# A fused embed, attention, state-space and expert kernel: maxima ahead of chain steps, the state projection behind its slot, the mask product first, a scatter awaited later

## What is computed

```python
h = concat(edges(x), (U * s @ Vt)[x_txt])
h = h + local_attention(norm(h))      # 16 heads of 16, window 128
h = h + routed_block(norm(h))         # gelu(x @ w_block) for the 288 tokens with the highest score
h = h + state_space(norm(h))          # h_t = A h_(t-1) + B u_t; A is a rotation in Fourier space
h = h + experts(norm(h))              # a shared feed-forward net, and the 2 best of 8 experts
```

## Time and profile before

| | |
|---|---|
| median of 3 runs | 2193.5 us |
| the profiled execution | 2192.07 us, of which the span is 2190.3 us |
| busy, share of the span | PE 90%, weight loads 71%, DVE 62%, ACT 49%, POOL 37% |
| granted TensorE clock, mean | 0.969 of full speed |
| passes 0 to 15 | about 69 to 1457 us; a loop pass takes 87.8 us |
| pass 16 and the hand-over to the experts | about 1457 to 1559 us |
| expert phase | about 1559 us to the end |

### The profile page before, as it was taken

The page is one execution under the profiler, slowest core; times in us unless marked ns, Lnnn a source line. Parts: engine busy times, 40 slices in busy tenths (PEclk is TensorE's granted clock), DMA queues, the critical chain, the costliest instruction groups (busy, mean ns, idle before and its releaser), DMA issues.

```text
span 2190.3 us, 44925 instructions
## 1 busy us (share of the span) xinstructions
PE 1965.9 (90%) x13651; PEld 1559.6 (71%) x13652; DVE 1350.6 (62%) x3572; ACT 1079.5 (49%) x2513; POOL 819.2 (37%) x1535
## 2 busy tenths in 40 slices
PE   2879999999999999999999999985789999999997
PEld 1546666666666666666666666653689999999997
DVE  5647668577576685775766757643455565555654
ACT  0336455455554554555545555541355455555553
POOL 3113324334243233342432333322344545454454
PEclk8789999999999999999999999996899999999998
DMA  4220211211202112112021121110333232323322
GB/s 138 65 58 9 66 45 29 65 35 45 65 15 65 44 28 65 33 47 65 15 65 43 30 65 31 35 59 8 111 84 84 44 83 47 81 48 81 48 47 40
DMA packets 81090, 116.53 MB, mean 53 GB/s; under 512 B 20965, under 2 KB 61509, under 8 KB 78725
## 3 DMA queue, kind: packets, MB, share of 16 engines
q1 hardware_dynamic: 54948, 85.34, 14.1%
q0 software_dynamic: 23360, 27.91, 7.8%
q10 hardware_dynamic: 2736, 2.76, 0.4%
HBM read 51.58 MB, written 26.71 MB: 36 GB/s over the span
## 4 chain that ended last, share of the span: by engine, by line
PE 51%; DVE 16%; issue 14%; POOL 8%; DMA 5%; ACT 4%; POOLq 0%; DVEq 0%; SPq 0%; ACTq 0%
PE ps L1780 10%; PE ps L1616 8%; POOL slot_rows L658 4%; PE ps L1493 4%; PE ps L1792 3%; PE ps L1791 3%; PE ps L1793 3%; DVE mx L1119 2%; PE ps L1582 2%; PE ps L1465 2%; DMA result<-yb,idx_o 2%; PE ps L1607 2%; PE ps L1561 2%; PE ps L1548 2%; DMA slot_rows<-pay,row_i 2%
## 5 line engine op out<-in xcount | busy, mean ns | idle before, releaser
L793 ACT ACTIVATE prob<-ps,mx 128x256 f32<-128x256 f32 (+1 forms) x768 | 295.0, 443 | 254.9 <-DVE mx L1119 240.1
L897 ACT ACTIVATE hid_hi<-ps,b 128x256 fp32r<-128x256 f32 x408 | 205.8, 504 | 286.1 <-PE ps L1780 286.1
L1119 DVE TENSOR_REDUCE mx<-ps 128x2 f32<-128x512 f32 (+1 forms) x384 | 224.5, 594 | 116.0 <-PE ps L1540 107.3
L785 ACT ACTIVATE pT<-ps 128x512 f32<-128x512 f32 (+1 forms) x384 | 205.2, 534 | 123.9 <-PE ps L1548 120.5
L1395 DVE TENSOR_TENSOR hid_lo<-hid_full,hid_hi 128x256 fp32r<-128x256 f32 x408 | 172.3, 426 | 150.7 <-ACT hid_full L900 150.1
L1539 PE MATMUL ps<-ks,qs 96*128 96x512 f32 (+1 forms) x384 | 186.7, 487 | 63.9 <-ACT prob L793 51.0
L1791 PE MATMUL ps<-w_hi,hid_hi 128*128 128x256 f32 x816 | 232.3, 285 | 0.0
L1792 PE MATMUL ps<-w_lo,hid_hi 128*128 128x256 f32 x816 | 227.9, 279 | 0.0
L1793 PE MATMUL ps<-w_hi,hid_lo 128*128 128x256 f32 x816 | 227.9, 279 | 0.0
L900 ACT ACTIVATE hid_full<-ps,b 128x256 f32<-128x256 f32 x408 | 206.2, 505 | 0.0
L1548 PE MATMUL ps<-ident,prob 128*128 128x128 f32 x1280 | 204.8, 277 | 0.0
(11 more groups left out here) (269 smaller groups left out, 4175.6 us busy)
## 6 DMA issues: line engine op xcount, KB each, us to landing
w_raw<-in_w SPq DMA_DIRECT2D x16, 1024.0 KB, 6.0
xin<-in_x SPq DMA_DIRECT2D x32, 384.0 KB, 3.6
qs<-q_hi SPq DMA_DIRECT2D x128, 96.0 KB, 2.1
ks<-k_hi SPq DMA_DIRECT2D x256, 48.0 KB, 2.1
qs<-q_lo SPq DMA_DIRECT2D x64, 96.0 KB, 2.1
ks<-k_lo SPq DMA_DIRECT2D x128, 48.0 KB, 2.1
xn_rows<-xc SPq DMA_DIRECT2D x16, 384.0 KB, 2.5
result<-h SPq DMA_DIRECT2D x16, 384.0 KB, 2.5
```

Of the source, the lines that this page charges most:

```text
L785: act.activation(pT[:, u % TB, :, k0:2, :], ps[:, 2 + u % 2, :].rearrange("p (h k q) -> p h k q", h=2, k=2)[:, :, k0:2, :], ACT.Copy).then ...
L793: ins = act.activation(prob[:, s % PB, hh, w], ps[:, s % 2, hh * 2 * P + w.start:(hh + 1) * 2 * P], ACT.Exp, bias=mx[:, s % 2, hh:hh + 1])
L897: act.activation(hid_hi[:, f], ps[:, f % 4, 0:CHUNK], ACT.Gelu_apprx_tanh, bias=b1[half][:, f:f + 1])
L1119: dve.tensor_reduce(mx[:, s % 2], sc, AX_X, ALU.max, negate=True).then_inc(max_done.sem, 1)
```

## The change

- DVE: in slots 14, 20 and 21 (`LATER`) the maxima of the unit come ahead of the chain's work; the statistics of the state-space sum move from slot 20 to 21.
- PE: the drive moves behind unit 14; the queries move ahead of the last PV product; the output product moves ahead of the PV product in slots 16 and 24; the mask product comes ahead of the score product in each bank; the first of the three products of `values_sum` moves to slot 1; `turn_chain(.., 0)` waits for bank 7 only ahead of its second half.
- Pass 16: POOL's `dispatch` moves behind the state-space work; `gate_ratio` and `slot_ranks` of the last item move to slot 30, ahead of seven of the eight upper products of the shared net; DVE's last `shared_sum` moves behind the fourth of the eight list copies, and PE waits for it ahead of the first chunk.
- Expert phase, POOL: the scatter of chunk `j - 1` is awaited behind the issue of the gather for chunk `j + 2`, in place of right behind its own issue.

```diff
+LATER = (STATE, OUT + 1, OUT + 2)
@@ POOL
-                if late:
+                if late and att:
                     dispatch(b - 2)
                 if chain:
                     chain_deviations(b - 1, 1)
                     direct_term(b - 1)
                     states(b - 1)
+                if late and not att:
+                    dispatch(b - 2)
...
-                pool.wait_ge(y_stored.sem, y_stored.at(j, 32))
-                pool.sem_inc(y_sent.sem, 1)
...
+            def rows_added(j):
+                pool.wait_ge(y_stored.sem, y_stored.at(j, 0))
+                pool.sem_inc(y_sent.sem, 1)
+
+            def rows_ahead(lo, hi):
                 with pool.Fori(lo, hi) as j:
                     gather_rows(j, 2)
+                    rows_added(j)
                     add_rows(j)
@@ ACT
+                    if first_weights and s == min(UPS):
+                        gate_ratio(b - 1)
                     for f in UPS.get(s, ()) if chain else ():
                         hidden_layer(b - 1, f)
...
-            gate_ratio(NB - 1)
@@ DVE
                     dve.wait_ge(h3_ready.sem, h3_ready.at(b, 1))
+                if s == OUT + 2:
                     chain_rows(b, 2)
...
-                    if chained:
+                    if chained and s not in LATER:
                         chain(b - 1, s)
...
                     if att:
                         unit(b, s)
+                    if chained and s in LATER:
+                        chain(b - 1, s)
...
-            shared_sum(NB - 1)
...
+                if e == 3:
+                    shared_sum(NB - 1)
@@ PE
-                    pe.matmul(dst, qs[:, r, m, i * P:(i + 1) * P], ks[:, r, :, m, keys], start=True, stop=False)
-                    pe.matmul(dst, ident_bf[:], mask_bf[:, :, c0:2 * P], start=False, stop=True
+                    pe.matmul(dst, ident_bf[:], mask_bf[:, :, c0:2 * P], start=True, stop=False)
+                    pe.matmul(dst, qs[:, r, m, i * P:(i + 1) * P], ks[:, r, :, m, keys], start=False, stop=True
                               ).then_inc(scores_done.sem, 1)
...
-                if n == 0:
-                    pe.wait_ge(hid_ready.sem, hid_ready.at(b, 0))
...
+                    if n == 0 and k == 1:
+                        pe.wait_ge(hid_ready.sem, hid_ready.at(b, 0))
...
-                if s == TURN1 + 2:
+            def drive(b):
...
+                    if head and s == TURN2 - 1:
+                        queries(b + 1)
                     if att and s == BLOCK:
-                        values_sum(b)
+                        values_sum(b, 1, NT)
...
                     if att:
                         unit(b, s)
+                    if att and s == TURN0:
+                        values_sum(b, 0, 1)
...
+                    if chained and s == TURN1 + 2:
+                        drive(b - 1)
...
+                    if last and s == min(UPS):
+                        slot_ranks(b - 1, False)
...
+            pe.wait_ge(h4_ready.sem, h4_ready.at(NB, 0))
             turn_chunk(0)
```

More of the change, by code:

```diff
@@ L1517, in values, with values_sum @@
                 ins.then_inc(proj_done.sem, 1)
-            def values_sum(b):
+            def values_sum(b, first, last):
                 pe.wait_ge(v_ready.sem, v_ready.at(b, 1))
                 pe.wait_ge(h1_ready.sem, h1_ready.at(b, 0))
-                for i in range(NT):
+                for i in range(first, last):
                     ins = pe.matmul(ps[:, 5, D:2 * D].rearrange("p (h d) -> p h d", h=NH), ones9[:], vaug[:, i, :, 0:DK],
                                     start=(i == 0), stop=(i == NT - 1))
-                ins.then_inc(sumv_done.sem, 1)
+                if last == NT:
+                    ins.then_inc(sumv_done.sem, 1)
             def unit(b, s):
@@ L1550, in unit @@
                     ins.then_inc(turned.sem, 1)
+                if s in WO:
+                    i = WO.index(s)
+                    pe.wait_ge(cxT_ready.sem, cxT_ready.at(b, i + 1))
+                    for k in range(KB):
+                        ins = pe.matmul(ps[:, 5, D:2 * D], cxT[:, k], wo[:, k], start=(k == 0), stop=(k == KB - 1))
+                    ins.then_inc(wo_done.sem, 1)
                 if PV <= s < NU + PV and (s - PV) % 2 == 1:
@@ L1577, in unit, with turn_chain @@
                     ins.then_inc(cx_turned.sem, 1)
-                if s in WO:
-                    i = WO.index(s)
-                    pe.wait_ge(cxT_ready.sem, cxT_ready.at(b, i + 1))
-                    for k in range(KB):
-                        ins = pe.matmul(ps[:, 5, D:2 * D], cxT[:, k], wo[:, k], start=(k == 0), stop=(k == KB - 1))
-                    ins.then_inc(wo_done.sem, 1)
             def tile_out(i):
                 return ps[:, 6 + i // 2, (i % 2) * D:(i % 2 + 1) * D]
-            def turn_chain(b, n, head):
+            def turn_chain(b, n, head, first=False):
+                if n == 0 and not first:
+                    pe.wait_ge(hid_ready.sem, hid_ready.at(b - 1, FB - 1))
                 pe.wait_ge(xc_ready.sem, xc_ready.at(b, n + 1))
                 pe.wait_ge(xcT_ready.sem, xcT_ready.at(b, n))
-                if n == 0:
-                    pe.wait_ge(hid_ready.sem, hid_ready.at(b, 0))
                 if n == 1:
@@ L1687, in logits, with sequence @@
                     ins.then_inc(logit_done.sem, 1)
-            def sequence(b, att, late, chained, head, first=False):
+            def sequence(b, att, late, chained, head, first=False, last=False):
                 for s in range(SLOTS):
-                    if first and s == 1:
+                    if first and not chained and s == 1:
                         pe.wait_ge(mats_read.sem, mats_read.at(0, 1))
@@ L1703, in sequence @@
                     if chained and s == TURN0:
-                        turn_chain(b - 1, 0, head)
+                        turn_chain(b - 1, 0, head, first)
                     if att:
                         unit(b, s)
+                    if att and s == TURN0:
+                        values_sum(b, 0, 1)
                     if late and s == RANKS:
@@ L1720, in sequence @@
                         turn_rows(b + 1)
-                    if head and s == TURN2 - 1:
-                        queries(b + 1)
                     if head and s == TURN2:
@@ L1746, in _ @@
             pe.wait_ge(late_loaded.sem, late_loaded.at(0, NLATE))
-            sequence(1, True, False, True, True)
+            sequence(1, True, False, True, True, first=True)
             with pe.Fori(2, NB - 1) as b:
@@ L1750, in _ @@
             sequence(NB - 1, True, True, True, False)
[L1751 to L1752 removed]
+            sequence(NB, False, True, True, False, last=True)
             for n in range(2 * NT):
```

12 lines of the change are left out of this document (6 added, 6 removed).

## The result

The changed kernel is slower: 2222.7 us (median of 4 runs, 2219.2 to 2226.4) against 2192.5 us for the kernel before (median of 4 runs, 2188.2 to 2195.5), ratio 1.014, 95% interval 1.0113 to 1.0166. The profiled execution took 2225.24 us with a span of 2223.5. The forecast was 2220.

A forecast was written before the change was run, and what follows sets the result against it. PE was taken as the bound, busy 82.12 of a pass's 87.80 us. Fourteen passes +52, passes 0 and 15 −2.5, first expert product −12.7, experts −9 gave +28 on 2192.07: 2220 us, range 2165 to 2262.

The forecast's parts named there:

- Start: Loop pass up to slot 14: shorter waits for turned rows and last hidden piece, score 14 about 0.75 us earlier.
- Drive: Loop pass, slots 14 to 16: about 4 us idle before unit 14, first edge product 3.1 us later, score 16 2.7 late.
- Mask first: Each unit's bank in a pass: 0.09 us less per wide unit, 1.7 us a pass, about 0.4 us of it counting.
- Slots 19 to 22: Loop pass: the 1.06 us wait before score 22 goes, `turn_rows` waits about 2 us, 0.7 us more to score 23.
- Slots 24 to 26: Loop pass end: output product and queries fill 1.4 us of waits, and 0.3 us of alignment goes.
- Clock: Loop pass: half-clock dip at the 4 us wait costs 1.55 us; one at `turn_rows` in six of ten passes, 0.7 us.
- Passes 0 and 15: Outside the regular loop passes: they keep the small gains, −2.5 us together (0 to −5).
- Pass 16: Moved dispatch gains 3.5 − 0.9 = 2.6 us; with moved ranks, first expert product starts 12.7 us sooner (8 to 14).
- Experts: Expert phase: PE's 10.0 us of waits for gathered rows and a 1 us clock dip go, −9 us (−4 to −11).
- No dip: Rival: the clock stays full in the loop, +20 us there and −24 outside, 2188 us; chance 0.15.
- The drive absorbed: Rival: DVE and edge products catch up before slot 20, a pass gains 2.9 us, total 2128 us; chance 0.18.
- Longer dips: Rival: PE at 1.2 GHz through slots 14 to 18 and from 22 on, +6 us a pass, 2252 us; chance 0.17.

The follow-up runs named there:

- e12: Changed kernel with the drive back ahead of unit 14 and DVE's loop order wholly as in the kernel before (LATER empty): 2129.0 us, ratio 0.971.
- e4: Kernel before with only the changes outside passes 0 to 15 (dispatch, gate ratio, ranks, shared sum, scatter): 2165.3 us, ratio 0.988.
- e8: Kernel before with only the mask product put ahead of the score product in each bank: 2183.1 us, ratio 0.996.
- e6: Changed kernel with the drive back ahead of unit 14 and DVE's slots 20 and 21 ordered as in the kernel before: 2131.4 us, ratio 0.972.
- e1: Changed kernel with the drive back ahead of unit 14 on PE, all else as changed: 2162.3 us, ratio 0.986.
- e3: Kernel before with only the drive moved behind unit 14 and DVE's products with u behind the maxima of slot 14: 2267.7 us, ratio 1.034.
- e5: Changed kernel with the drive back ahead of unit 14 and DVE's statistics of slot 21 moved behind the normalised rows (xn): 2148.2 us, ratio 0.979.
- e11: Changed kernel with only DVE's slots 20 and 21 back in the order of the kernel before, drive still behind unit 14: 2214.1 us, ratio 1.010.
- e2: Changed kernel with an extra, unawaited run of the drive ahead of unit 14, besides the one behind it: 2208.9 us, ratio 1.008.
- e9: e6 with the statistics put behind the maxima of slot 22, the sum still ahead of the maxima of slot 20: 2144.0 us, ratio 0.977.
- e7: Kernel before with only the expert phase changed, a chunk's scatter awaited behind the next gather: 2176.0 us, ratio 0.992.
- e10: e6 with the statistics put between the maxima of slots 20 and 21, the sum still ahead of both: 2130.3 us, ratio 0.971.

## Why the prediction came out

The sign, the size (2222.7 against 2220) and the mechanism at slot 14 were right. That the size came out so close is luck: the fourteen loop passes cost 57 us where 52 were forecast, passes 0 and 15 cost 7.6 us where a gain of 2.5 was, and the experts gained 19.7 where 9 were. So I go through the sum.

*The balance, in medians.* e12 has all of the change but the drive's place and DVE's order: −63.5 us. Of that, e4's ends are −27 and e8's mask order −9; the moves of projections, turned rows and value sums hold what is left, about −27, that is (87.82 − 0.36 − 85.61) × 14 = 26 by the passes, if the three add up. Putting the maxima of slots 20 and 21 first adds 31 (e6 to e1), the drive behind the unit 60 (e1 to the changed kernel), the maxima of slot 14 first nothing (e12 to e6, +2). −63.5 + 2.4 + 30.9 + 60.4 = +30.2 us. (These steps run from kernel to kernel, so they add up by construction; each by itself is a difference of two medians.)

*Start: −0.75.* From the start of the pass to score 14 it is 35.64 us, before 36.29: −0.65. Right.

*Drive: 4 us idle, the edge products 3.1 us later, score 16 2.7 late.* The wait is 3.71 us. At score 20 the changed pass is 5.7 − 0.65 = 5.1 us late; less the 2.3 us of half clock 2.8. The wait of the edge product is 1.16 us, in the 1 to 1.5 of the prediction. e3 shows it on the kernel before, e1 takes it away. Right.

*Mask first: 0.09 us a wide unit, 0.4 a pass on the path.* From the first product of a bank to the transposes it is 0.45 us now (mask at 731.04, transposes 731.49), where 0.55 was needed, and e8 has the 0.36 a pass. The Trainium skill ("TensorE: Matmul & The Clock Gate", Part 2) says that PE pulls weight loads ahead of matmuls in flight, and I had taken from it that the edit might be worth nothing. The measurement decides against that reading of it. That the saving is the bare load is read from the rows; e8 shows the size, not the cause.

*Slots 19 to 22: +0.7.* The exchange of a wait of 1.06 for one of about 2 us was right (1.85), and its price at full clock too (0.5 in the changed kernel, slot 20 to `turn_rows` 6.80 against 6.32; 0.9 in e6 against e1).

*Slots 24 to 26: −1.7.* −1.18, from `turn_rows` to the end of the pass (26.78 against 27.96). The waits for `pT` went as forecast; 0.3 us of what I had put to alignment, and 0.2 more, did not come. At full clock that makes 2.0 us a pass instead of 1.4.

*Clock: 1.55 for the dip at score 14 and 0.7 for one at `turn_rows` in six passes of ten.* The sum was right by luck, 2.25 against 2.3 us, and both terms were wrong. I took the dip's length from pass 15 (3.4 us); it was 6.8 us, of which 5.1 held work, in eleven passes (3.4 us in the first three). And the second never came. It is no invention: in e1 it comes in eight passes of twelve and costs 1.54 us, in e5 and e6, where the wait for `xn` is 0.53 us or none, never. What failed is the step that priced the two waits one by one. In the changed kernel the clock has fallen at score 14 and is whole again 23 us before the wait for `xn` begins, and this same wait leaves it alone. Whether the earlier fall is the reason, no run shows: in e1 the same wait lets the clock fall in some passes and not in others that are alike up to it. The Trainium skill ("TensorE: Matmul & The Clock Gate", "HAM oscillation") tells of a loop with waits of about 3 to 5 us whose clock falls at every one of them. The wait of 3.7 us at score 14 agrees with that, in all fourteen passes; the wait of 1.85 us is shorter than those of the page, and brought a fall in e1 in nine passes of fourteen and here in none.

Sum of a pass: 3.7 forecast, 4.35 measured in the last eleven and 2.4 to 3.6 in the first three, taken from router product to router product: 52 and 57.4 us in fourteen.

*Passes 0 and 15: −2.5.* This term failed outright, by 10 us. Of the 64.9 us lost by pass 16, 57.4 are those of the fourteen passes, 1.4 lie ahead of pass 1's router product and 6.2 in pass 15, from its router product on. In pass 15 the clock fell in a second place, for 10 us:

```profile
1500.60:1513.60 13.00, 11.76 (x53) 8.96 (x46) 5.91 (x29) 3.66 (x6) 1.39 (x2) 0.61 0.09 32
```

Before, that pass had one fall. I had carried over the loop's gains without asking what its new waits (2.5, 2.3, 1.5 and 1.2 us) would do. What brought the second fall can be read from the experiments. From router product to router product, the changed kernel and then e11, which differs from it in DVE's slots 20 and 21 alone:

```profile
1439.77:1523.42 83.65, 72.24 (x464) 52.98 (x469) 47.10 (x137) 41.70 (x94) 24.35 (x58) 0.92 0.13 44
1423.74:1501.36 77.62, 67.47 (x464) 49.11 (x469) 46.23 (x137) 41.92 (x94) 24.42 (x58) 0.98 0.15 48
```

e11 has the waits of 2.5 and 2.3 us too, and one fall of 3.4 us. The second fall stands in the kernels whose statistics of the state-space sum come in slot 21 or later (the changed one, e1, e2, e5, e9: 81 to 84 us) and in none of those that have them in slot 20 (the kernel before, e3, e4, e6, e7, e8, e10, e11, e12: 76 to 79 us). e6 and e9 differ in nothing but the place of these statistics. So it is the later statistics that cost pass 15 its 6 us.

*Pass 16: dispatch −3.5 + 0.9, first expert product −12.7.* Up to POOL's first deviations 3.4 us were gained. Then the dispatch took its new place with a first DMA of 2.87 us, where it was 1.12, next to DVE's split of the second weights (3.08 us from 1558.26), and POOL came to the second deviations 3.2 us behind the statistics, where it had been 0.2: of the gain 1.3 us was left, 2.1 us lost instead of 0.9. In all ten profiled kernels with the dispatch there this first DMA takes 2.87 us, begins 1.1 us behind the start of the split and ends 0.88 us behind its end; in the four others it takes 1.12 us. That it waits for the split is read from this overlap, and no run parted the two. Ranks, table and shared sum went as forecast (the wait of 10.73 us is 0.70 now), and the first expert product gained 12.0.

*Experts: −9.* The term was mis-sized by half: 19.7 us in the changed kernel. e7 gives 14.0 to the edit. Read from waits it was 10.0 and 1 for the clock, of which I took 9 for caution. Read from the chunks it was more: ten of them took 12.4 to 17.6 us among those of 11.7 to 11.9, 14 us above them in all, of which e7 keeps 2 in three chunks. The trace of before also has two stretches at half clock there, up to 1565 and from 1609 to 1613. The rest, about 5 us, is a difference that doesn't follow the edit. The starts of chunks that follow each other, PE in e3, in its earlier and then its later part:

```profile
1843.10 0.60 PE L1769 MATMUL ps<-ident,xg 128*128 128x128 f32 x4
1854.75 0.60 PE L1769 MATMUL ps<-ident,xg 128*128 128x128 f32 x4
...
1998.51 0.60 PE L1769 MATMUL ps<-ident,xg 128*128 128x128 f32 x4
2010.36 0.60 PE L1769 MATMUL ps<-ident,xg 128*128 128x128 f32 x4
2022.03 0.60 PE L1769 MATMUL ps<-ident,xg 128*128 128x128 f32 x4
```

A chunk takes 11.65 us in the one, and 11.85 and 11.67 by turns in the other. The kernel before, e1, e5, e6 and e7 were profiled in the second rhythm throughout, the changed kernel, e2, e4 and e9 to e12 in the first, e3 and e8 in both. So the new order of the expert phase is found with either rhythm (e4 and e7), and so is the old one (e3). It is worth 0.2 us in every other chunk, 5 us an execution, and no edit here sets it.

The rivals. *No dip* (2188) fell by e2 and by the windows. *The drive absorbed* (2128) fell at its own test, the wait for `rot` of 1.16 us, over the 1 us from which it should decide. *Longer dips* (2252) was half right: twice the length at score 14, but only there.

## What to carry to other kernels

Work that stands inside a wait is free only there. The profile before showed it, 2.75 us of drive and 1.09 us of wait behind it: moving the one opened the other to 3.71 us, and delayed what needed the moved result besides. A wait named in a profile is worth removing only if what it waits for isn't on the same engine's chain as the next thing awaited: the 1.06 us ahead of score 22 came back as 1.85 us in the changed kernel and as 1.01 us in e10, since DVE had as much work ahead of `xn` in either order. And a bundle of edits is worth taking apart: of this one, all that was moved on DVE was worth nothing or less, one move on PE cost 60 us, and the remainder gains 63.

## What the runs showed of the hardware

Whether a wait of PE lets the clock fall isn't told by its length alone. The same 1.85 us for `xn` came with half clock in nine of fourteen passes of e1 and in none of the changed kernel, where the clock had fallen and was whole again 23 us earlier; what decides between them stays open. The same 3.7 us ahead of score 14 came with 3.4 and with 6.8 us of half clock within one execution of e11, and of the changed kernel. In dense work a fall of 3.4 us cost 1.54 us; one of 6.8 us, of which PE stood still for 1.7, cost 2.3. Filling the wait with eight products that nobody needs kept the clock whole and made the pass 2.3 us shorter (e2).

An indirect DMA that POOL issued 1.1 us behind the start of a DVE product of two operands (3.08 us) took 2.87 us instead of 1.12, in all ten kernels that have the two side by side.

A loop of identical chunks can run in two rhythms 0.1 us apart on the mean (11.65, or 11.85 and 11.67 by turns) and change from one to the other within an execution. In this kernel that moves the total by 5 us, 0.2%, and a single profile of either kernel would have put it to the change.
